# Cross-attention and state-space kernel: the last two keys leave the PV matmuls and go by broadcast, ScalarE and GpSimd; loads cut into pieces; the context stage reordered

## What is computed

```python
xq = layernorm(x) * g1 + beta1 ; xk = layernorm(ctx) * g1 + beta1
q, k, v = xq @ Wq.T + bq, xk @ Wk.T + bk, xk @ Wv.T + bv      # 8 heads of 64
attn = softmax(q @ k.T / 8)                                   # 4096 x 3202 per head
x = x + (attn @ v) @ W_o.T + b_o
U = (layernorm(x) * g2 + beta2) @ W_in.T @ Bmat               # 64 wide
s_t = silu(s_{t-1} @ A.T) + U_t                               # over 4096 tokens
x = x + s @ Cmat + mean(ctxb) @ W_prog.T + b_prog
```

## Time and profile before

| | |
|---|---|
| median of three runs | 2306.91 us |
| the profiled execution | 2304.2 us, its span 2302.2 us, mean granted TensorE clock 0.992 |
| context stage, 144 to 324 us | TensorE busy nearly throughout until 313 us |
| unit 0 | 324.0 to 396.0 us |
| units 1 to 31 | 396.0 to 2108.4 us |
| output stage | 2108.4 to 2245 us |
| scan and end | 2245 to 2302.2 us |
| busy in the span | PE 2246.0 us, DVE 1714.8, ACT 1104.2, POOL 1583.9 |

### The profile page before, as it was taken

The page is one execution under the profiler, slowest core; times in us unless marked ns, Lnnn a source line. Parts: engine busy times, 40 slices in busy tenths (PEclk is TensorE's granted clock), DMA queues, the critical chain, the costliest instruction groups (busy, mean ns, idle before and its releaser), DMA issues.

```text
span 2302.2 us, 36166 instructions
## 1 busy us (share of the span) xinstructions
PE 2246.0 (98%) x14264; PEld 1303.6 (57%) x14264; DVE 1714.8 (74%) x2084; ACT 1104.2 (48%) x1415; POOL 1583.9 (69%) x1039
## 2 busy tenths in 40 slices
PE   8999989999999999999999999999999999999987
PEld 8998864555555545555555555555555555445664
DVE  5865446888878887888888788888888888854666
ACT  3654423444545454545444444545454454453454
POOL 1200016888888888888888888888888888888322
PEclk8999989999999999999999999999999999999999
DMA  6660225677677777777777777777776777778633
GB/s 242 213 193 10 83 64 109 148 157 170 152 161 158 162 172 172 171 160 157 159 160 170 173 172 175 159 157 156 165 161 152 156 165 161 183 184 188 225 120 146
DMA packets 159703, 365.02 MB, mean 159 GB/s; under 512 B 23535, under 2 KB 63087, under 8 KB 158894
## 3 DMA queue, kind: packets, MB, share of 16 engines
q0 software_dynamic: 59904, 218.13, 46.4%
q1 hardware_dynamic: 99630, 144.59, 19.5%
HBM read 95.41 MB, written 49.02 MB: 63 GB/s over the span
## 4 chain that ended last, share of the span: by engine, by line
PE 77%; POOL 8%; issue 6%; DMA 5%; DVE 3%; ACT 1%; POOLq 0%; SPq 0%; DVEq 0%; ACTq 0%
PE ps L1365 27%; PE ps L1238 10%; PE ps L1340 7%; PE ps L1342 7%; PE ps L1344 7%; POOL accp L545 5%; PE ps L1202 4%; DMA acca<-pt 4%; PE ps L1332 3%; PE ps L1220 3%; PE ps L1210 3%; PE ps L1430 2%; PE ps L1183 1%; DVE mx_part L928 1%; PE ps L1192 1%
## 5 line engine op out<-in xcount | busy, mean ns | idle before, releaser
L727 ACT ACTIVATE pt<-ps 128x1024 f32<-128x1024 f32 x800 | 779.3, 1021 | 905.3 <-PE ps L1344 887.5
L545 POOL TENSOR_TENSOR accp<-accp,pt 128x1024 f32<-128x1024 f32 x416 | 1041.1, 2503 | 221.0 <-ACT pt L727 216.9
L928 DVE TENSOR_REDUCE mx_part<-ps 128x2 f32<-128x1024 f32 x768 | 937.9, 1221 | 340.1 <-PE ps L1238 340.1
L1365 PE MATMUL ps<-pt,v 128*64 128x512 f32 x3328 | 805.9, 605 | 0.0
L1001 DVE TENSOR_TENSOR ps<-ps,shb 128x1024 f32<-128x1024 f32 x403 | 493.1, 1223 | 48.4 <-PE ps L1344 48.4
L1365 PEld LDWEIGHTS ps<-pt,v 128*64 128x64 f32 x3328 | 201.9, 136 | 344.6 <-issue 335.6
L1238 PE MATMUL ps<-kk,qh 64*128 64x512 f32 x1536 | 349.6, 451 | 9.6 <-DVE mx_part L928 9.6
L1238 PEld LDWEIGHTS ps<-kk,qh 64*128 64x128 f32 x1536 | 143.4, 183 | 355.1 <-DVE mx_part L928 267.6
L1340 PE MATMUL ps<-qh,kk 64*128 64x512 f32 x1664 | 329.1, 391 | 2.9 <-ACT pt L727 2.8
L1342 PE MATMUL ps<-qh,kk 64*128 64x512 f32 x1664 | 329.0, 390 | 0.0
L1344 PE MATMUL ps<-ql,kk 64*128 64x512 f32 x1664 | 328.8, 390 | 0.0
(11 more groups left out here) (158 smaller groups left out, 1864.3 us busy)
## 6 DMA issues: line engine op xcount, KB each, us to landing
acca<-pt POOLq DMA_DIRECT2D x224, 512.0 KB, 4.9
accb<-pt POOLq DMA_DIRECT2D x160, 512.0 KB, 4.9
q_scratch<-kk SPq DMA_DIRECT2D x32, 512.0 KB, 4.4
acca<-accp POOLq DMA_DIRECT2D x32, 512.0 KB, 4.6
o_scratch<-ost SPq DMA_DIRECT2D x32, 512.0 KB, 3.0
og<-o_scratch SPq DMA_DIRECT2D x32, 512.0 KB, 5.9
shb<-m_scratch SPq DMA_DIRECT2D x31, 512.0 KB, 4.1
xs<-x SPq DMA_DIRECT2D x16, 512.0 KB, 6.4
```

Of the source, the lines that this page charges most:

```text
L545: nc.gpsimd.tensor_tensor(acc[:, :], acc[:, :], pt[n % PT_SLOTS][:, :], ALU.add).then_inc(added_p, 1)
L727: nc.scalar.activation(pt[n % PT_SLOTS][:, :], src, ACT.Exp, scale=SCALE).then_inc(exped, 1)
L928: nc.vector.tensor_reduce(mx_part[:, m % QT, :, m // QT], src, AX_X, ALU.max).then_inc(max_taken, 1)
L1365: ins = mm(ps[HD * h:HD * (h + 1), 6, :], v[:, t, f:f + HD], pt[n % PT_SLOTS][:, h * QB:(h + 1) * QB], start=(t == 0), stop=(t == NT - 1))
```

## The change

(1) The tile of two keys is no longer a PV tile and no longer in the GpSimd sum. ScalarE makes exp for its two partitions only; SP sends these two rows to HBM (`t_scratch`), reads them back broadcast over partitions (`tailb`) and once into `den8`; ScalarE multiplies by V's two rows, kept as columns (`v_tail`), and GpSimd adds the two products to `oraw`. (2) The row maxima are `mx_row`, 128 x 8, one transpose instead of four; the shift goes as 8 x 128 to HBM and back into `sh`. (3) Eight maxima pieces of unit 1 move from unit 0 into the context stage, the two short pieces move from step 8 to step 0 (`M_ORDER`); K is projected in the order of `PAIR_ORDER`, the last group's K before its V. (4) K of the later pairs is loaded in 13 pieces of 256 KB over eight units instead of 4 of 832 KB over four; W_O in four pieces over four units, x and b_o a unit or more earlier. (5) In the output stage two small TensorE products and what follows stand one group later, group 1's `norm2_scale` stands ahead of the next `add_x`, and `out` is stored in 32 pieces. A small activation stands ahead of all others on ScalarE.

```diff
-M_FIRST = NM + 2 * M_LEAD
+M_EARLY = NM + 2 * M_LEAD
+M_ORDER = [*range(2 * M_LEAD), NM - 2, NM - 1, *range(2 * M_LEAD, NM - 2)]
...
-    return [(i // NM + 1, i % NM) for i in range(first, min(last, NM * (UNITS - 1)))]
+    first = M_EARLY + 2 * (NJ * u + j)
+    return [(i // NM, M_ORDER[i % NM]) for i in range(first, min(first + 2, NM * UNITS))]
...
+def ctx_maxima(g):
+    if g < 2:
+        return []
+    if g == C_G - 1:
+        return [(0, m) for m in range(21, NM)]
+    third = [(1, g - 3)] if 3 <= g < C_G - 2 else [(0, 20)] if g == C_G - 2 else []
+    return [(0, 2 * (g - 2)), (0, 2 * (g - 2) + 1)] + third
...
 # SP
+            def send_shift(w):
+                sp.wait_ge(shift_ready, w + 1)
+                wait(sp, sh_loaded, 16 * (w - 1))
+                wait(sp, shb_loaded, 16 * (w - 2))
+                sp.dma_start(m_scratch[w % 2].rearrange("h (q k) -> (h q) k", k=P), shift_row[:, :].bitcast(F32)).then_inc(sh_stored, 16)
+                sp.wait_ge(sh_stored, 16 * (w + 1))
+                sp.dma_start(sh[w % 2][0:HD + 1:HD, :].bitcast(F32), m_scratch[w % 2]).then_inc(sh_loaded, 16)
...
+            def send_tail(u):
+                n = NT * u + NT - 1
+                sp.wait_ge(exped, n + 1)
+                wait(sp, tail_loaded, 32 * (u - 1))
+                wait(sp, den8_loaded, 80 * u)
+                sp.dma_start(t_scratch[u % 2], pt[n % PT_SLOTS][0:TAIL_KEYS, :]).then_inc(tail_stored, 16)
+                sp.wait_ge(tail_stored, 16 * (u + 1))
+                wait(sp, o_scaled, u)
+                for h in (0, 1):
+                    sp.dma_start(tailb[HD * h:HD * (h + 1), :, :],
+                                 t_scratch[u % 2:u % 2 + 1, :, h * QB:(h + 1) * QB].to_broadcast([HD, TAIL_KEYS, QB]))\
+                        .then_inc(tail_loaded, 16)
+                wait(sp, rden_ready, u)
+                sp.dma_start(den8[:, 1:1 + TAIL_KEYS, :], t_scratch[u % 2].rearrange("k (p j) -> p k j", j=8)).then_inc(den8_loaded, 16)
...
-                pi, part = u // BLOCKS + 1, u % BLOCKS
+                pi, part = u // BLOCKS + 1, 2 * (u % BLOCKS)
...
                 if u > 0:
+                    send_tail(u - 1)
                     fold_den(u - 1)
                     spread_rden(u - 1)
                 if u + 1 < UNITS:
+                    send_shift(u + 1)
                     spread_shift(u + 1)
...
             for d in range(2, X_G):
+                if d == 4:
+                    send_tail(UNITS - 1)
...
 # GpSimd
+            def add_tail(u):
+                pool.wait_ge(tail_scaled, u + 1)
+                pool.wait_ge(o_taken, u + 1)
+                for k in range(TAIL_KEYS):
+                    wait(pool, tail_added, TAIL_KEYS * u + k)
+                    nc.gpsimd.tensor_tensor(oraw[:, :], oraw[:, :], tailb[:, k, :], ALU.add).then_inc(tail_added, 1)
...
-                    else:
+                    elif t in P_TILES:
                         add_tile(u, t)
+                    if t == 10 and u > 0:
+                        add_tail(u - 1)
...
                 add_bias(d)
+                if d == 8:
+                    add_tail(UNITS - 1)
...
 # ScalarE
+            def scale_tail(u):
+                p = unit(u)[1]
+                if u == 0:
+                    act.wait_ge(v_tail_loaded, 16 * PAIRS * TAIL_KEYS)
+                act.wait_ge(tail_loaded, 32 * (u + 1))
+                for k in range(TAIL_KEYS):
+                    ins = nc.scalar.activation(tailb[:, k, :], tailb[:, k, :], ACT.Copy, scale=v_tail[:, p, k:k + 1])
+                ins.then_inc(tail_scaled, 1)
...
                     if j == 4 and u > 0:
+                        scale_tail(u - 1)
                         take_den(u - 1)
...
 # VectorE
             def invert(u):
-                dve.wait_ge(den8_loaded, 64 * (u + 1))
+                dve.wait_ge(den8_loaded, 80 * (u + 1))
                 wait(dve, rden_stored, 16 * u)
-                nc.vector.reciprocal(rden8[:, :], den8[:, :]).then_inc(rden_ready, 1)
+                nc.vector.tensor_reduce(rden8[:, :], den8[:, :, :].rearrange("p k j -> p j k"), AX_X, ALU.add).then_inc(den_summed, 1)
+                dve.wait_ge(den_summed, u + 1)
+                nc.vector.reciprocal(rden8[:, :], rden8[:, :]).then_inc(rden_ready, 1)
...
-                if d + 1 < X_G - 1:
+                root_first = d == 1 or d == X_G - 2
+                if d + 1 < X_G and not root_first:
                     add_x(d + 1, 0)
...
 # TensorE
-                for q in range(QT):
-                    ins = nc.tensor.transpose(ps[0:HD + 1, 7, q * P:(q + 1) * P], mxp[:, q, :], ident[:, :])
-                ins.then_inc(max_turned, 1)
+                if w == 0:
+                    pe.wait_ge(n_ready, 2 * NG)
+                nc.tensor.transpose(ps[0:2 * QT, turn_bank(w), 0:P], mx_row[:, :, :].rearrange("p h q -> p (h q)"), ident[:, :])\
+                    .then_inc(max_turned, 1)
...
                 if t == 0:
-                    pe.wait_ge(shift_ready, u + 1)
+                    pe.wait_ge(sh_loaded, 16 * (u + 1))
...
+                if t == NT - 1:
+                    return
...
-                if d == 7:
+                if d == 8:
                     pe.wait_ge(cb_summed, 2)
```

More of the change, by code:

```diff
@@ L93, with nth_max @@
 MOD_LO = 96
+def ctx_maxima(g):
[5 more added lines that the diff above has]
+    return [(0, 2 * (g - 2)), (0, 2 * (g - 2) + 1)] + third
+EARLY = [p for g in range(C_G) for p in ctx_maxima(g)]
+def nth_max(w, m):
+    return EARLY.index((w, m)) if (w, m) in EARLY else NM * w + M_ORDER.index(m)
 def wait(eng, sem, value):
@@ L467, in _ @@
                 if u + 1 < UNITS:
+                    send_shift(u + 1)
                     spread_shift(u + 1)
+                if 2 <= pi < PAIRS and part + 1 < K_PARTS:
+                    load_k(pi, part + 1)
                 if u > 0:
@@ L1245, in maxima, with early_maxima @@
                 ins.then_inc(max_done, 1)
+            def early_maxima(pairs):
+                for w, m in pairs:
+                    pe.wait_ge(k_ready, FC * (C_G - 1 if m >= NM - 2 else 2 * (m // QT) + 1) + 1)
+                    maxima(w, m)
             def turn_max(w):
@@ L1392, in _ @@
                     for w, m in todo[:1]:
-                        maxima(w, m, m)
-                    if added(u, 2 * j + 1):
+                        maxima(w, m)
+                    if u == 0 and j == 0:
+                        for t in (0, 1):
+                            open_tile(u, t)
+                            scores(u, t, True, False)
+                        for t in (0, 1):
+                            shift_scores(u, t, False)
+                    elif added(u, 2 * j + 1):
                         open_tile(u, 2 * j)
@@ L1398, in _ @@
                         scores(u, 2 * j + 1, True, True)
+                        scores(u, 2 * j, False, True)
                     else:
                         score_tile(u, 2 * j)
-                    for w, m in todo[1:-1]:
-                        maxima(w, m, m)
-                    if added(u, 2 * j + 1):
-                        scores(u, 2 * j, False, True)
-                    else:
                         score_tile(u, 2 * j + 1)
-                    if ahead and j == turn_step(u):
+                    if ahead and j == TURN_STEP:
                         turn_max(u + 1)
-                    for w, m in todo[max(1, len(todo) - 1):]:
-                        maxima(w, m, m)
+                    for w, m in todo[1:]:
+                        maxima(w, m)
                     if j > 0:
```

300 lines of the change are left out of this document (169 added, 131 removed).

## The result

The changed kernel has a median of 2279.01 us in four runs (2277.44 to 2279.64), beside 2308.34 us for the kernel before in the same series (2303.46 to 2310.59). The ratio is 0.9875 with a 95% interval of 0.9857 to 0.9893: 29 us faster, where 57 were forecast and 2238 to 2273 was the range. The profiled execution has a span of 2277.7 us against 2302.2, so the spans differ by 24.5, less than the medians: the profiled execution before took 2304.2 us, 4 under its median, the one after 2279.56, at its median.

The account below looks back on a forecast made before the run. TensorE and VectorE were both taken to bound an ordinary step. Terms 34 + 17 - 0.4 - 3 + 2 + 1.3 + 4 = 55 us off 2304.2 gave 2249, stated as 2250 us; range 2238 to 2273.

Parts of the forecast that it names:

- forecast 33: Units 1 to 30: gain of 34 from step 0, step 8 and the transposes, minus 3 for denominators, plus 2 for K loads.
- Rival (c): Step 0 does not shrink, as a wait of exp or O's bank takes the tile's place; 2272 us, chance 0.06.
- step 9: The transposes' step in each unit, 4.93 us before; three of four transposes leave, gain taken as 0.45 us.
- the 3 us for late denominators: Units: ScalarE's scalings delay the denominators VectorE inverts; 0.1 us per unit, 3 in all.
- (a): Rival: VectorE waits for the denominators in every unit, up to 0.9 us each, 28 us; 2276 us, chance 0.10.
- (b): Rival: GpSimd's sums become the bound and exp waits for slots, 1 us per unit; 2280 us, chance 0.12.
- +2: Units: smaller K pieces shorten GpSimd's waits in the eight units that had the large load; gain 2 us.
- forecast 17: Unit 0: 72.0 us falls to 55.1 with all 13 steps at two maxima pieces or fewer; gain 17 us.
- the fall of the clock that I allowed for: Unit 0: if TensorE's clock still falls for two steps, the gain is 14 us, not 17.
- forecast -0.4: Context stage: nine more maxima pieces lose 5.4 us, the last group's new order gains 5.0.
- forecast +1.3: Last unit: the last PV tile goes, 0.9 us, and 0.4 of step 0's gain.
- forecast +4: Output stage: `sum_ctx` wait gone 3.4, `norm2_scale` first and output in halves 1.5, `send_tail` -1, `add_tail` -1.

Follow-up runs that it names:

- e3: Changed kernel with the even tile's first product taken ahead of the odd tile's scores in step 1 of each unit; 2271.62 us.
- e4: Changed kernel with half of tile 0's exp (the second head's 512 columns) left out in every unit but the first; 2271.19 us in one run.
- e1: Changed kernel with only the order of the maxima put back, so the two short pieces are in step 8 again; 2287.1 us.
- e2: Changed kernel with only the tail keys' path put back: TensorE's product with V and GpSimd's sum again; 2275.6 us.
- e8: Changed kernel with K loaded in four pieces of 832 KB again, at their old place; 2294.33 us in one run.
- e11: Changed kernel with the tail path put back as in e2 and K in four pieces of 832 KB; 2285.37 us in one run.
- e12: As e8, but SP issues each 832 KB K piece at the end of its unit's list; 2278.82 us in one run.
- e6: Changed kernel with SP's `og` loads in the last unit moved behind the tail rows of unit 30; 2271.31 us.
- e7: Changed kernel with the last unit's two tail keys sent through TensorE's product and GpSimd's sums again; 2272.4 us.
- e9: Changed kernel with the edits of e3, e6 and e7 joined, and the first root chain behind the addition again; 2259.12 us.
- e10: As e9, but the first root chain stands ahead of the addition, as in the changed kernel; 2259.02 us.

## Why the forecast was right in direction and too large

The sum itself had a slip. The terms for the output stage are 3.4 + 1.5 - 1 - 1 = 2.9, not 4, and 2249 with the 2.7 of the median is 2252, not 2250: by its own terms the forecast was 2253.

**Units 1 to 30: forecast 33, measured 22.1.** The step that failed: "VectorE's chain for 3.39. I take the larger: step 0 goes from 4.13 to 3.39, a gain of 0.74". The size of step 0 was right, 3.48 from shift to shift (gain 0.67). The error was to weigh two chains when a third was close: exp of tile 1 ends 4.1 us after the unit's start, and the scores of tile 3 want its banks 0.57 after step 1's start. A step 0 shorter than about 3.56 hands the rest on to step 1, 0.29 per unit or 8.7 us in 30. e3 and e4 show that wait, e1 and e2 show that it is not there without the short step. Rival (c) had named a wait of exp that takes the tile's place; it came one step later and took 0.29 of 0.67, not all. The rest of the shortfall is small: step 9 gave 0.37 instead of 0.45 (2.4 us), step 0 0.67 instead of 0.74 (2.1 us), and the step that had the short pieces lost 0.06 instead of 0.04. Against these, the last step of a unit is 0.06 shorter from shift to shift, since a short piece opens the next one, and the 3 us for late denominators stayed out.

**The PV tile and the order of the pieces.** That both bound a step and one alone gives nothing was my reading of rows 2, and e1 and e2 bear it out: 0.05 for either, 0.67 for both.

**Denominators and GpSimd's sums, rivals (a) and (b).** VectorE's waits ahead of the sum of the denominators are "DMA den<-den_sb: 1.1, 3" over all 32, so (a) did not come, and the 3 us I took for it neither. GpSimd waits much longer ahead of its last accumulate (L643, rows of the view by line):

```profile
L643 POOL DMA_DIRECT2D acca<-accp x32: 876/878/920, 388.6 to 2091.4; - x32
...
  DMA acca<-pt: 92.9, 25
```

That is 3.7 us each, more than the 3 I had allowed for, and 92.9 us in all where the same line before has 36.0 in 13; but ordinary steps stay at 4.13 to 4.17, and only one step of units 1 to 30 is over 4.9 us (5.56, in unit 12): the wait is covered, and (b) did not come in the ordinary unit. e8 shows how near it is: one large load ahead of the tail rows makes a step of 9.15 us.

**K's pieces.** I took +2 for them. Against the kernel before nothing shows: the step in which these waits fall (step 4) has a mean of 4.23 us over units 1 to 30 in both. Against e8 they are worth 18.7 us, of which e11 finds 7.6 without the tail path. So in the main they repair what the tail rows on the same queue would break, and e12 shows that the place does it as well.

**Unit 0: forecast 17, measured 15.5.** Ordinary steps take 4.38 against the 4.36 that I used; the mechanism held, and TensorE does not wait for `sh`. The first step takes 3.3 instead of 2.5, with a wait of 0.81 for VectorE's reduction in it. The granted clock over the unit is 1.00, before it was 0.95; so the fall of the clock that I allowed for did not come in this unit, and its absence is part of the gain.

**Context stage: forecast -0.4, measured -3.1.** The rows split it. The last group's work began at 301.48 and could begin at 307.77 now, 0.43 behind the piece at 307.34: 6.3 lost where I had 5.4. Of this 0.6 is the first group, which takes 12.75 us instead of 12.11. From there to unit 0 it was 23.1 us and is 19.9, a gain of 3.2 where I had 5.0. That is the term that was mis-sized, and 1.6 of the missing 1.8 is the clock. Of the two V projections of the last group, alike in work (12 matmuls), the first takes 4.59 us:

```profile
307.34 0.49 PE L1352 MATMUL ps<-kk,qh 64*128 64x512 f32 x2
...
318.89 4.59 PE L1323 MATMUL ps<-wkv,n 128*128 128x512 f32 x12
...
324.42 3.03 PE L1323 MATMUL ps<-wkv,n 128*128 128x512 f32 x12 [0.83 <-ACT v L732]
```

The windows view has the granted clock as its eighth figure; 0.52 is the lower level, 1.2 GHz:

```profile
318.90:322.40 3.50, 3.50 (x11) 2.79 (x10) 0.91 (x2) 0.00 (x0) 0.00 (x0) 0.52 0.85 296
```

Of the thirteen kernels here with this context stage four have this slow projection; the other nine take 1.4 to 1.6 us less from the last transposes of `xs` to unit 0. So without it the stage loses about 1.5. (The kernel before has the lower level there too, 0.51 from 318 to 326 us, but among waits for VectorE.)

The start of unit 0 also varies among the thirteen, from 322.5 to 327.9 us, by the granted clock between 50 and 100 us (0.90 to 0.95). That is not the reason here, for the kernel before has the same 0.91 as the changed one, and both begin the context stage at the same time (143.84 and 143.93). The rows are of the kernel before and of the changed one:

```profile
50.00:100.00 50.00, 50.00 (x397) 49.85 (x398) 34.46 (x105) 29.25 (x56) 9.25 (x8) 0.91 0.55 174
```

```profile
50.00:100.00 50.00, 50.00 (x394) 49.85 (x395) 34.40 (x105) 29.18 (x56) 8.79 (x8) 0.91 0.55 173
```

**Unit 31: forecast +1.3, measured -4.1.** The part failed that I had not costed: "SP stands some 4 us in `send_tail`" was written for the output stage, while in unit 31 the same small store stands behind 2 MB of loads. It took 9.7 us; line 381's slowest small transfer before was 5.5, and I used its median. e6 takes back 4.5.

**Output stage: forecast +4, measured -5.8.** The step that failed is "So `add_tail` here can stop VectorE's root chain twice more, 2 x 1.0 = 2 us; I take half, -1". VectorE's chain was stopped, but by the additions of `xb`, for 5.2 us, and TensorE stood behind it: e7, without the last unit's tail path, has 4.2 us less of this wait and none of the 1.8 that the lower clock takes. That `norm2_scale` goes first, which I had among the gains of 1.5, gives nothing by e9 and e10; at this place it costs 1.6. By the start of group 4 the stage is 7.5 us behind the kernel before (31.0 against 23.5). "Against that SP stands some 4 us in `send_tail` ahead of group 4's loads, and ScalarE 1.3: -1" was right in the time, 4.7 us, but the rows show no cost of it.

From group 4 to group 15 the change gains 4.4. The 3.4 for `sum_ctx` did come, TensorE no longer waits there, but its waits for `nt` rose from 8.8 to 10.1 (the view of waits after the change, us in total, times, longest). From group 15 to the end 2.8 are lost (77.8 against 75.0): the wait for `xn` rose from 1.8 to 3.4, and the granted clock of the scan and the end is 0.91 instead of 0.96. What of the 2.8 belongs to which stays open.

```profile
PE ps L1578 <- ACT nt L873: 10.1, 7, 2.7
```

On the stop itself: the row at 2091.60 shows one operation on four elements at 3.30 us beside GpSimd additions of 2.83 for two instructions, where 1.21 was the longest of rows 10. By the Trainium skill, "SBUF — State Buffer", section "SBUF: two separate sides", whichever of the two starts first holds the shared port pair for its whole instruction and the other waits. That VectorE waits the trace agrees: the operation ends at 2091.60 + 3.30 = 2094.90, and the two GpSimd additions at 2092.03 + 2.83 = 2094.86. But it waited through two instructions, where in rows 10 it was one.

## What to carry to other kernels

When one step is made shorter than its neighbours, list every resource that the next step reuses, not only the two longest chains: here the banks freed by exp bound as soon as step 0 fell below about 3.56 us, 0.6 under its 4.13, while 0.74 was to be taken from it, and moving one product ahead of them gave 7.4 us. A small transfer on a queue costs what stands ahead of it; put the large loads behind it or cut them, and look at each place where the order of the queue differs, the last unit above all. A path that saves work in the steady state can be dropped for the last round, where less covers its latency. Before a loss is put down to the clock of an early stretch, look whether the kernel before had the same clock there.

## What the runs showed of the hardware

- A store of 8 KB held its queue for 9.7 us behind 2 MB of loads, for 7.4 us behind one load of 832 KB (e8), for 3.8 us behind one of 256 KB, for 3.1 (e12) and 2.0 us (e6) with none of these directly ahead.
- One VectorE operation on 128 x 4 elements took 3.30 us beside GpSimd's additions, where the same line has a median of 0.17 us; it ended 0.04 us behind two additions, not one.
- With a wait of 5.5 us TensorE's granted clock was 0.52 from 2097 to 2104 us, the lower level, and the 24 matmuls behind the wait took 7.51 us; behind waits of 1.33 (e7) and 1.53 us (e10) the same 24 took 5.71 and 5.72.
- The first matmul pair that follows a gap of 0.15 us lasts 0.51 instead of 0.40, so the short wait of step 1 costs 0.26.
- The start of unit 0 varies by 5.4 us among thirteen kernels with the same context stage: it is at 322.5 and 322.6 us where the granted clock between 50 and 100 us is 0.95 (e1, e9), from 325.0 to 327.9 where it is 0.90 to 0.93.
